# Two turns and the first two finishes moved at the end of a mixture of experts

## The reference

```python
scores = jax.nn.sigmoid(xf @ gate_w + bias)
top_scores, top_idx = jax.lax.top_k(scores, K)          # K = 2 of 8
...
up = jnp.einsum('th,ehi->tei', xf, up_w) + up_b         # 128 -> 512
hact = jax.nn.gelu(up, approximate=False)
eo = jnp.einsum('tei,eih->teh', hact, down_w) + down_b  # 512 -> 128
combined = jnp.einsum('teh,te->th', eo * 0.1, w)
shared = (jax.nn.gelu(xf @ sw_up + sb_up, approximate=False) @ sw_down + sb_down) * 0.1
out = (shared + combined).reshape(b, s, h)
out = out / (jnp.max(jnp.abs(out), axis=-1, keepdims=True) + 1e-06)
...
x = x + out
```

## Time and profile before

| | us |
|---|---|
| median of 3 runs | 1177.02 (1176.69 to 1177.24) |
| the profiled execution | 1179.81 |
| its span | 1178.2 |
| PE busy in the span | 1086.2 (92%) |
| DVE busy | 906.3 (77%) |
| ACT busy | 712.5 (60%) |
| POOL busy | 402.2 (34%) |

### The profile page before, as it was taken

One profiled execution on the slowest core, in us unless ns is written; L12 is line 12 of the kernel. 1 busy time (PEld: TensorE's weight loads), 2 busy tenths in 40 slices (PEclk: granted clock), 3 DMA queues, 4 the chain that ended last, 5 costly groups with the idle time before them and its releaser, 6 DMA issues. The chain is left out here.

```text
span 1178.2 us, 18881 instructions
## 1 busy us (share of the span) xinstructions
PE 1086.2 (92%) x7015; PEld 559.0 (47%) x7015; DVE 906.3 (77%) x1588; ACT 712.5 (60%) x1208; POOL 402.2 (34%) x254
## 2 busy tenths in 40 slices
PE   5599889999999999999979999999999889999996
PEld 4256665445555555555413222222212367888885
DVE  7968477866666667667777899999999268787777
ACT  5324537433334454533267888888878778888783
POOL 0147410867677776778522200000010011221200
PEclk9599999999999999999979999999999989999998
DMA  4000010000000000100010110000010012222111
GB/s 97 1 1 3 1 37 1 1 11 1 1 1 2 2 1 1 55 27 1 1 45 15 55 42 26 18 17 26 15 20 1 1 37 83 81 66 95 37 36 36
DMA packets 30658, 29.36 MB, mean 25 GB/s; under 512 B 10784, under 2 KB 26280, under 8 KB 29544
## 3 DMA queue, kind: packets, MB, share of 16 engines
q1 hardware_dynamic: 30568, 28.17, 8.1%
HBM read 23.57 MB, written 4.26 MB: 24 GB/s over the span
## 5 line engine op out<-in xcount | busy, mean ns | idle before, releaser
L2041 ACT ACTIVATE narrow_att_probs<-psum 128x512 f32<-128x512 f32 x512 | 265.0, 603 | 66.8 <-PE psum L1964 66.6
L2082 DVE TENSOR_REDUCE front_maxima<-psum 128x1 f32<-128x1024 f32 x240 | 281.9, 1219 | 21.9 <-PE psum L1048 17.6
L1293 POOL TENSOR_TENSOR gated_tally<-gated_probs,gated_tally 128x1024 f32<-128x1024 f32 x96 | 231.0, 2406 | 77.5 <-ACT gated_probs L1559 69.0
L1559 ACT ACTIVATE gated_probs<-psum 128x1024 f32<-128x1024 f32 x128 | 124.1, 1022 | 159.5 <-PE psum L1440 156.9
L1661 DVE TENSOR_REDUCE gated_maxima<-psum 128x1 f32<-128x512 f32 x256 | 164.6, 685 | 50.2 <-PE psum L1330 49.0
L1964 PE MATMUL psum<-narrow_att_q,narrow_att_k 50*128 50x512 bf16 x448 | 146.7, 386 | 5.2 <-ACT narrow_att_probs L2041 4.7
L1048 PE MATMUL psum<-narrow_att_k,narrow_att_q 48*128 48x512 bf16 x448 | 133.1, 383 | 11.1 <-DVE front_maxima L2082 2.5
L1977 PE MATMUL psum<-narrow_att_probs,narrow_att_v_ones 128*32 128x512 f32 x1024 | 138.8, 615 | 0.1
L2548 DVE TENSOR_TENSOR moe_hidden_lo<-moe_hidden,moe_hidden_hi 128x512 fp32r<-128x512 f32 x144 | 104.5, 751 | 42.0 <-ACT moe_hidden_hi L2455 41.5
L1453 PE MATMUL psum<-gated_probs,gated_values 128*64 128x512 f32 x512 | 132.1, 610 | 0.0
L2451 ACT ACTIVATE moe_hidden<-psum,back_up_bias 128x512 f32<-128x512 f32 x144 | 96.4, 689 | 33.5 <-PE psum L73 33.5
(11 more groups left out here) (408 smaller groups left out, 1961.0 us busy)
## 6 DMA issues: line engine op xcount, KB each, us to landing
moe_mixb<-moe_mix_scratch SPq DMA_DIRECT2D x8, 1024.0 KB, 5.1
narrow_parts_scratch<-gated_values SPq DMA_DIRECT2D x12, 128.0 KB, 2.1
narrow_parts_scratch<-narrow_att_part SPq DMA_DIRECT2D x12, 128.0 KB, 2.2
narrow_att_q<-narrow_parts_scratch SPq DMA_DIRECT2D x14, 96.0 KB
narrow_att_q<-narrow_parts_scratch SPq DMA_DIRECT2D x42, 32.0 KB
narrow_att_k<-narrow_parts_scratch SPq DMA_DIRECT2D x14, 96.0 KB
narrow_att_k<-narrow_parts_scratch SPq DMA_DIRECT2D x42, 32.0 KB
X<-in_L_attn_inputs SPq DMA_DIRECT2D x4, 256.0 KB, 4.1
```

The costliest lines, as they stand in the source:

```text
L1293: pool.tensor_tensor(tally[:, n % 2, :, :], probs[:, kt % 4, :, :], so_far, ALU.add).then_inc(tallied, 1)
L1559: act.activation(probs[:, k % 4, :, :], psum[:, 2 * e:2 * e + 2, :], ACT.Exp, scale=SCALE).then_inc(exped, 1)
L2041: act.activation(probs[:, k % 3, 2 * e + u % 2, :], psum[:, SCORE_BANK + j % 3, :], ACT.Exp, scale=SCALE).then_inc(exped, 1)
L2082: dve.tensor_reduce(maxima[:, n % 2, at:at + 1], chunk.rearrange("p a b -> p (a b)"), AX.X, ALU.max).then_inc(chunk_used, 1)
```

## The change

Two places change, one on PE and one on DVE. On PE the two turns that stand inside the loop move by one product each: turn(0) goes ahead of down(33) instead of behind it, and turn(1) ahead of down(34). On DVE finish(0) moves from behind acc(34) to behind acc(33), which is ahead of the four instructions of low(35). finish(1) moves from behind acc(35) to behind acc(34), ahead of add_term(35). finish(2) and finish(3) stay last. No instruction is added or dropped, and ACT, POOL and SP keep their order.

```diff
@@ tensor engine, in the loop over k
                 if k == GATES_AT:
                     gate_logits()
+                if k - 2 >= (ALLE - 1) * QUARTERS:
+                    turn_back((k - 2) % QUARTERS)
                 if k >= 1:
                     down(*steps[k - 1])
...
                 if k == MIX_AT:
                     turn_mix()
-                if k - 2 >= (ALLE - 1) * QUARTERS:
-                    turn_back((k - 2) % QUARTERS)
@@ vector engine, in the loop over k and behind it
                 if k >= 1:
                     add_term(k - 1)
-            finish(0)
+
+                if k - 2 >= (ALLE - 1) * QUARTERS:
+                    finish((k - 2) % QUARTERS)
             add_term(ALLE * QUARTERS - 1)
-            for q in range(1, QUARTERS):
+            for q in range(QUARTERS - 2, QUARTERS):
                 finish(q)
```

## The result

| | before | after |
|---|---|---|
| median, 22 runs each | 1176.84 us (1173.79 to 1179.55) | 1174.51 us (1170.86 to 1176.49) |
| span of the profiled execution | 1178.2 us | 1174.6 us |
| PE, DVE, ACT busy | 1086.2, 906.3, 712.5 us | 1085.2, 905.3, 712.6 us |

The ratio is 0.9978, with an interval of 0.997 to 0.9986: faster by 0.22%, or 2.6 us, and by 1.6 to 3.5 us with the interval (the two medians differ by 2.33 us). The forecast, 2.12 us or 0.18%, lies in the interval, and so does the bound of 0.2%.

The account below looks back on a forecast made before the run. PE bounds most of the kernel, DVE's queue the last 12 us. One finish leaves its end, 2.18 us, and 0.06 come back: 2.12 us off the median of 1177.02 gives 1174.9 us, range 1174.2 to 1176.0.

Parts of the forecast that it names:

- the bound of 0.2%: Whole run: line between no change and a change, 2.35 us; the forecast lay 0.23 us inside it.
- DVE's queue sets the end: Last 12 us: DVE runs without a gap after low(35), so one finish less there saves 2.18 us.
- The 0.06 us that were to come back: DVE, term(34): start delayed 0.06 us by the later down(34), taken off the 2.18 us gain.
- The turns are free where they stand: PE ahead of down(33) and down(34): no wait for acc, 0.68 and 1.11 us to spare; ACT's step 35 doesn't move.
- finish(1) moved ahead of add_term(35): nothing: DVE behind acc(34): finish(1) changes places with equal work in a full queue and gains nothing by itself.
- the second rival: End of DVE's queue: both finishes leave it, gaining 4.30 us, to 1172.7; chance 3%.
- The cover is nearly full: DVE ahead of low(35): finish(0)'s 2.18 us use up gaps of 1.97 us, leaving low(35) 0.04 us late.
- Beside ACT finish(0) isn't stretched: DVE, finish(0) beside ACT's gelus: no stretch taken, 2.18 us long; 1.00 us kept for the range.
- the side to which I had given 20%: Whole run: measured gain above 2.35 us, 20 of the forecast's 85%, since 2.12 us and the scatter are close.

Follow-up runs that it names:

- finish(0) alone: Changed kernel with finish(1) left behind acc(35), so on DVE only finish(0) moves; tail 20.14 us, against 18.74 changed and 20.94 before.
- The three traces with ACT and POOL: Changed kernel with the last part of finish(1), or of finish(1) and finish(2) (coarse, then tile by tile), on ACT and POOL: 1173.46, 1174.56, 1173.77 us.
- the experiment: Kernel before with five unused largest-magnitude instructions (3.05 us) added on DVE behind acc(33); tail 21.67 us, 0.74 more.
- the finishes alone: Changed kernel with PE's turns put back as before, DVE as changed; tail 18.76 us, timed 1174.70 us, ratio 0.9981.
- the turns alone: Changed kernel with DVE's finishes put back as before, PE's turns as changed; tail 20.93 us.

## Why the prediction was right or wrong

**DVE's queue sets the end: right.** One finish less in it is 2.18 us, and the tail lost 2.20.

**The 0.06 us that were to come back: did not.** I had taken the 0.51 us between a last matmul and ACT's gelu for DVE too. DVE is quicker: with finish(0) alone its term(35) starts at 1160.79, 0.43 us behind the start of down(35)'s last matmul:

```profile
1160.36 0.39 PE L73 MATMUL psum<-moe_hidden_hi,back_down_lo 128*128 128x512 f32 x1
```

So term(33) and term(34) kept their places. In the changed kernel they start 0.45 and 0.46 us behind their last matmuls (1155.90 and 1161.91). The three traces with ACT and POOL, where term(35) waits for down(35) too, have the same 0.43 us.

**The turns are free where they stand: right**, and, beyond what I wrote, not needed either. The rows of before held this: turn(0) had ended at 1157.67, and finish(0) wanted it at 1159.10.

**"finish(1) moved ahead of add_term(35): nothing": wrong.** The step compared the new order with the old one, in which a finish covers the same spot, and not with the order that has finish(0) moved alone. I had all its terms: acc(34) ends at 1165.2 on the clock of before, and down(35) is seen at 1166.10 + 0.43 = 1166.5. The gap of 1.30 us that finish(0) alone leaves is just that. My total was right because the sum was made for both moves, and there I had compared down(35) with term(35) at 1167.38; the split was wrong, by 1.40 of 2.20 us. What I wrote against the second rival, that the rows show no gap there, was true of the rows and not of the queue: the gap opens only when finish(0) leaves.

**The cover is nearly full: right.** 0.61 us more cost 0.54 us. I forecast low(35) 0.04 us late; it was not late, and the room was 2.26 us by the experiment, against 1.97 us by adding up the gaps (the idle notes run from an end to a start, while DVE's instructions back to back overlap: a block of 0.69 us is followed after 0.60. From start to start the three gaps hold 1.25, 0.49 and 0.50 us, which is 2.24).

**Beside ACT finish(0) isn't stretched: right**, 2.19 us (1157.74 to 1159.93), with ACT in its gelus from 1157.11 on. But the two rows that I gave for it don't carry it. I wrote that a term takes 0.74 us "whether ACT works or not", at 1157.71 and at 1163.75. ACT was idle both times: it idled 1.49 us ahead of 1158.48, and its last instruction ended at 1163.03. The row that would have done is term(32) at 1152.12, 0.74 us with gelus from 1152.45. The choice of nothing rested on less than I said.

**The size.** 1174.9 us forecast, 1174.51 measured. By the ratio the gain is 2.6 us, beyond the bound of 2.35 us, on the side to which I had given 20%; but the interval, 1.6 to 3.5 us, has both sides in it, and doesn't tell 2.12 us from a size somewhat smaller or larger. The 20% rested on the scatter of three runs, 0.55 us. Over 22 runs the kernel before scatters by 5.8 us, and the measurement can't place 2.2 us on one side of a bound of 2.35 us; the tail in the trace can, and puts what the change itself is worth at 2.20 us, or 0.19%. The second trace of the same order on DVE, with the finishes alone, gives 2.18 us.

## What to carry to other kernels

Work at the end of a full queue is worth moving into an idle stretch of the same queue; but what it covered where it stood has to be listed too, and a second piece may have to move up to cover it. Judge each move against the order in which only the other has been made, not against the old one. Where runs scatter by more than the change is worth, measure from a mark in the trace just ahead of the change.

## What the runs showed of the hardware

The execution ahead of the changed stretch scatters by far more than the tail. The first matmul of up(0) is the same in all four profiled kernels below, and so is all that lies ahead of it. By the timeline of PE it began in the kernel before at

```profile
958.01 0.99 PE L71 MATMUL psum<-moe_UH,back_up_hi 128*128 128x512 f32 x1
```

in the changed one at

```profile
956.24 0.99 PE L71 MATMUL psum<-moe_UH,back_up_hi 128*128 128x512 f32 x1
```

with the turns alone at

```profile
954.47 0.99 PE L71 MATMUL psum<-moe_UH,back_up_hi 128*128 128x512 f32 x1
```

and with three instructions added to the kernel before at

```profile
954.42 0.99 PE L71 MATMUL psum<-moe_UH,back_up_hi 128*128 128x512 f32 x1
```

That is 3.6 us, while the tails of the three with the old order of finishes are 20.94, 20.93 and 20.93 us. Where ahead of it the scatter arises was not looked into. In the 22 runs of the changed kernel the time goes with PE's mean granted clock: it was 0.979 in the three fastest (1170.86 to 1171.24 us) and 0.973 in the four slowest (1176.01 to 1176.49 us). Which of the two follows from the other isn't shown.

DVE's addition of epsilon, 128x4, took 0.52 instead of 0.17 us beside POOL's addition, in both runs that had it, and POOL's 128x512 addition took 1.64 us when it came while DVE was in acc(35), and 1.26 us when it came while DVE was in L2584, which has one of its inputs in PSUM. The Trainium skill, page "SBUF — State Buffer", section "Who interferes with whom", says that whoever issues first gets the shared port pair for its whole instruction while the other blocks. The trace agrees that both can be held up: when DVE's addition of epsilon came, at 1166.05, 0.49 us of POOL's instruction were left, and it ended 0.03 us behind POOL's end.
